# Cross-attention: both halves of the values product side by side, half of k a step ahead, v between the turns

## What is computed

```python
def _L0_xattn_ref(query, key_value, Wq, bq, Wk, bk, Wv, bv, Wo, bo):
    ...
    q = (query @ Wq + bq).reshape(B, Nq, H, D).transpose(0, 2, 1, 3)
    k = (key_value @ Wk + bk).reshape(B, Nkv, H, D).transpose(0, 2, 1, 3)
    v = (key_value @ Wv + bv).reshape(B, Nkv, H, D).transpose(0, 2, 1, 3)
    attn = jnp.einsum('bhqd,bhkd->bhqk', q, k) * scale
    ...
    attn = jax.nn.softmax(attn, axis=-1)
    x = jnp.einsum('bhqk,bhkd->bqhd', attn, v).reshape(B, Nq, Cq)
    return x @ Wo + bo
...
x = x + _L0_xattn_ref(_layernorm(x, axis=-1), ctx_768, ...)
```

## Time and profile before

| | us |
|---|---|
| median of 3 runs | 1132.66 |
| lowest and highest run | 1132.36, 1137.8 |
| the profiled execution: its time | 1139.23 |
| its span, first to last instruction | 1137.4 |
| busy in it: PE, PEld, DVE, ACT, POOL | 1018.0, 876.5, 782.9, 654.5, 689.1 |

### The profile page before, as it was taken

The page is one execution under the profiler, slowest core; times in us unless marked ns, Lnnn a source line. Parts: engine busy times, 40 slices in busy tenths (PEclk is TensorE's granted clock), DMA queues, the critical chain, the costliest instruction groups (busy, mean ns, idle before and its releaser), DMA issues. The chain is left out here.

```text
span 1137.4 us, 30097 instructions
## 1 busy us (share of the span) xinstructions
PE 1018.0 (89%) x9432; PEld 876.5 (77%) x9433; DVE 782.9 (69%) x2353; ACT 654.5 (58%) x1517; POOL 689.1 (61%) x813
## 2 busy tenths in 40 slices
PE   5899999999999998797999728999999537999998
PEld 3698999998999977686788516778887526998997
DVE  7576776677667776564666589766766486777784
ACT  3466666666676651534778577556665373444541
POOL 2487777777777780445899417776777203655443
PEclk9899999999999997899999759999999767999999
DMA  5221122212222112890000511233233348545601
GB/s 161 70 63 60 55 79 71 67 56 60 74 61 78 60 46 93 223 351 1 1 0 1 94 70 34 47 46 55 47 51 51 93 149 258 146 117 176 136 6 11
DMA packets 68551, 94.33 MB, mean 83 GB/s; under 512 B 12764, under 2 KB 48048, under 8 KB 68496
## 3 DMA queue, kind: packets, MB, share of 16 engines
q1 hardware_dynamic: 52464, 73.02, 20.2%
q0 software_dynamic: 16032, 20.62, 11.0%
HBM read 73.69 MB, written 22.18 MB: 84 GB/s over the span
## 5 line engine op out<-in xcount | busy, mean ns | idle before, releaser
L1921 POOL DMA_INDIRECT e_x<-rows,source x71 | 76.0, 1071 | 101.3 <-ACTq L1758 35.9
L652 ACT ACTIVATE xa_pr<-xa_pr,xa_nm 128x257 f32<-128x257 f32 x256 | 109.6, 500 | 21.7 <-DVE xa_nm L701 21.7
L635 ACT ACTIVATE xa_kT<-xa_kvp,xw_bk 128x258 fp32r<-128x258 f32 x128 | 60.8, 476 | 91.0 <-PE xa_kvp L465 83.7
L694 DVE TENSOR_SCALAR_CACHE_REDUCE xa_pr<-xa_sc 128x257 f32<-128x257 f32 x256 | 98.0, 421 | 13.6 <-PE xa_sc L490 9.0
L1932 POOL DMA_INDIRECT out_x<-e_y,target x32 | 54.0, 1688 | 77.3 <-DVE e_y L2719 65.5
L1926 POOL DMA_INDIRECT base<-e_y,place x39 | 76.7, 1968 | 35.5 <-DVE e_y L2209 21.9
L2610 ACT ACTIVATE e_h<-e_hb,rc_F_b 128x512 f32<-128x512 f32 x64 | 44.0, 688 | 91.1 <-PE e_hb L2556 90.4
L2556 PE MATMUL e_hb<-e_xTs,e_w1s 128*128 128x512 f32 x384 | 92.3, 401 | 1.9 <-issue 1.9
L597 POOL TENSOR_TENSOR xa_ol<-xa_om,xa_tl 128x256 f32<-128x256 f32 x64 | 46.6, 728 | 75.5 <-DVE xa_rinv L724 75.3
L2572 PE MATMUL e_yb<-e_w2s,e_hTs 128*128 128x256 f32 x768 | 89.5, 278 | 0.0
L705 DVE TENSOR_SCALAR xa_pT<-xa_ptp 128x512 f32<-128x512 f32 x128 | 87.3, 682 | 1.8 <-PE xa_ptp L500 1.6
(11 more groups left out here) (365 smaller groups left out, 3009.4 us busy)
## 6 DMA issues: line engine op xcount, KB each, us to landing
e_w<-in_F_W SPq DMA_DIRECT2D x16, 1024.0 KB
w<-in_W SPq DMA_DIRECT2D x24, 512.0 KB, 9.8
xa_ctx<-in_ctxT SPq DMA_DIRECT2D x32, 257.0 KB, 3.2
xa_ctx<-in_ctxT SPq DMA_DIRECT2D x64, 128.5 KB, 3.2
xa_vb<-vlx SPq DMA_DIRECT2D x64, 128.0 KB
rows<-xs_oT SPq DMA_DIRECT2D x4, 516.0 KB, 10.0
xs_oT<-in_x SPq DMA_DIRECT2D x4, 512.0 KB, 4.1
base<-xs_oT SPq DMA_DIRECT2D x4, 512.0 KB, 3.2
```

The source lines that it names most:

```text
L652: act.activation(pr[:, par, g, :], pr[:, par, g, :], ACT.Exp, bias=nm[:, par, g:g + 1], scale=-1.0).then_inc(exp_ready, 1)
L694: dve.tensor_scalar(pr[:, par, g, :], sc[:, g, 0:S], CLAMP, None, ALU.min, ALU.min, accum_out=mx[:, par, g:g + 1]).then_inc(clip_ready, 1)
L1921: return pool.indirect_dma_start(out=out, out_offset=None, in_=rows, in_offset=bass.IndirectOffsetOnAxis(ap=index, axis=0))
```

## The change

On every engine the change reorders what a step does, and leaves the work the same.

- PE: `project_k` does one half a call. Half 1 of k(b+1) stands right behind the scores, half 0 of k(b+2), a step ahead, behind the second turn; `project_v(b+1)` stands between the two turns; `turn_output` and both halves of `values` then stand in one block before the next scores.
- ACT: only half 1 of `high_k(b+1)` ahead of the exponentials; half 0 of `high_k(b+2)` last.
- DVE: all four `clip` instructions in one block, then `store_output`, `bounds`, and behind them the copies of the probabilities and `rest_k`.
- POOL: `rest_of_context(b+2)` moves from the end of the step to right behind `normalise`, ahead of the queries.
- k(1) half 0 is projected, split and stored ahead of the first step. SP's list is the same.

```diff
--- before.py
+++ after.py
@@ -447,22 +447,21 @@
         def _(pe):
             pe.wait_ge(w.loaded, w.total)
 
-            def project_k(b, par):
-                pe.wait_ge(ch_ready, b * 2 + 2)
-                pe.wait_ge(cr_ready, b + 1)
+            def project_k(b, par, h):
+                if h == 0:
+                    pe.wait_ge(ch_ready, b * 2 + 2)
+                    pe.wait_ge(cr_ready, b + 1)
+                    pe.wait_ge(kh_ready, b * 2)
+                    pe.wait_ge(kl_ready, b * 2)
+                else:
+                    pe.wait_ge(v_ready, b)
                 high, rest = cs[:, par, 0], cs[:, par, 1]
-                for h in range(2):
-                    if h == 0:
-                        pe.wait_ge(kh_ready, b * 2)
-                        pe.wait_ge(kl_ready, b * 2)
-                    else:
-                        pe.wait_ge(v_ready, b)
-                    out, c = kvp[:, (par + h) % 2, 0:SE], slice(P * h, P * h + P)
-                    pe.matmul(out, wks[:, 0, c], high[:, 0, :], start=True, stop=False)
-                    pe.matmul(out, wks[:, 0, c], rest[:, 0, :], start=False, stop=False)
-                    pe.matmul(out, wks[:, 1, c], high[:, 0, :], start=False, stop=False)
-                    pe.matmul(out, wks[:, 2, c], high[:, 1, :], start=False, stop=False)
-                    pe.matmul(out, wks[:, 3, c], rest[:, 1, :], start=False, stop=True).then_inc(kp_ready, 1)
+                out, c = kvp[:, (par + h) % 2, 0:SE], slice(P * h, P * h + P)
+                pe.matmul(out, wks[:, 0, c], high[:, 0, :], start=True, stop=False)
+                pe.matmul(out, wks[:, 0, c], rest[:, 0, :], start=False, stop=False)
+                pe.matmul(out, wks[:, 1, c], high[:, 0, :], start=False, stop=False)
+                pe.matmul(out, wks[:, 2, c], high[:, 1, :], start=False, stop=False)
+                pe.matmul(out, wks[:, 3, c], rest[:, 1, :], start=False, stop=True).then_inc(kp_ready, 1)
 
             def project_v(b, par):
                 pe.wait_ge(kh_ready, b * 2 + 1)
@@ -527,28 +526,31 @@
 
             def step(b, par, slot):
                 scores(b, par)
+                if not static(b) or b < B - 1:
+                    project_k(b + 1, 1 - par, 1)
                 if not static(b) or b >= 1:
                     turn(b - 1, 1 - par, 0)
                 if not static(b) or b < B - 1:
-                    project_k(b + 1, 1 - par)
+                    project_v(b + 1, 1 - par)
                 if not static(b) or b >= 1:
                     turn(b - 1, 1 - par, 1)
+                if not static(b) or b < B - 2:
+                    project_k(b + 2, par, 0)
                 if not static(b) or b >= 2:
                     turn_output(b - 2, par)
                 if not static(b) or b >= 1:
                     values(b - 1, 1 - par, (2 * slot + par + 3) % 4, 0)
-                if not static(b) or b < B - 1:
-                    project_v(b + 1, 1 - par)
-                if not static(b) or b >= 1:
                     values(b - 1, 1 - par, (2 * slot + par + 3) % 4, 1)
 
             pe.wait_ge(wh_ready, 6)
             pe.wait_ge(wl_ready, 4)
             pe.wait_ge(rows_zeroed, 2)
-            project_k(0, 0)
+            project_k(0, 0, 0)
+            project_k(0, 0, 1)
             pe.matmul(ptp[0:B, 0:D], cl[:, 0, :], wv[:, 0, :], start=True, stop=False)
             pe.matmul(ptp[0:B, 0:D], cl[0:64, 1, :], wv[0:64, 1, :], start=False, stop=True).then_inc(vlp_ready, 1)
             project_v(0, 0)
+            project_k(1, 1, 0)
             run_steps(pe, step, 0, B)
             turn(B - 1, 1, 0)
             turn(B - 1, 1, 1)
@@ -603,6 +605,8 @@
             def step(b, par, slot):
                 if not static(b) or b >= 2:
                     normalise(b - 2, par)
+                if not static(b) or b < B - 2:
+                    rest_of_context(pool, o, b + 2, par, 1 - slot)
                 if not static(b) or b >= 1:
                     pool.wait_ge(exp_ready, b * 4)
                 if not static(b) or b < B - 1:
@@ -610,8 +614,6 @@
                 if not static(b) or b >= 1:
                     last_probability(b - 1, 1 - par)
                     last_value(b - 1, 1 - par, (2 * slot + par + 3) % 4)
-                if not static(b) or b < B - 2:
-                    rest_of_context(pool, o, b + 2, par, 1 - slot)
                 if static(b):
                     c = b if b < 4 else b - B + 8
                     x = xs[:, T // 8 * c:T // 8 * c + T // 8, :]
@@ -663,16 +665,18 @@
                 if not static(b) or b < B - 2:
                     high_context(b + 2, par, 1 - slot)
                 if not static(b) or b < B - 1:
-                    high_k(b + 1, 1 - par, 0)
                     high_k(b + 1, 1 - par, 1)
                 exponentials(b, par)
                 if not static(b) or b < B - 1:
                     store_v(b + 1, 1 - par, (2 * slot + par + 1) % 4)
+                if not static(b) or b < B - 2:
+                    high_k(b + 2, par, 0)
 
             act.wait_ge(ones_ready, 4)
             high_k(0, 0, 0)
             high_k(0, 0, 1)
             store_v(0, 0, 0)
+            high_k(1, 1, 0)
             run_steps(act, step, 0, B)
 
         @block.vector
@@ -735,24 +739,25 @@
                     mask_output(b - 2, par)
                     invert(b - 2, par)
                 clip(b, par, 0)
+                clip(b, par, 1)
                 if not static(b) or b >= 3:
                     store_output(b - 3)
+                bounds(b, par)
                 if not static(b) or b >= 1:
                     store_probabilities(b - 1, 1 - par, 0)
-                clip(b, par, 1)
                 if not static(b) or b < B - 1:
-                    rest_k(b + 1, 1 - par, 0)
-                bounds(b, par)
+                    rest_k(b + 1, 1 - par, 1)
                 if not static(b) or b >= 1:
                     store_probabilities(b - 1, 1 - par, 1)
-                if not static(b) or b < B - 1:
-                    rest_k(b + 1, 1 - par, 1)
+                if not static(b) or b < B - 2:
+                    rest_k(b + 2, par, 0)
 
             rest_k(0, 0, 0)
             rest_k(0, 0, 1)
             dve.wait_ge(vlp_ready, 1)
             dve.tensor_tensor(vl[:], ptp[0:B, 0:D].unsqueeze(1).to_broadcast([B, 4, D]), maskj[:],
                               ALU.mult).then_inc(vl_ready, 1)
+            rest_k(1, 1, 0)
             run_steps(dve, step, 0, B)
             mask_output(B - 2, 0)
             invert(B - 2, 0)
```

## The result

| | before | after |
|---|---|---|
| median of 4 runs | 1134.31 us | 1172.33 us (1171.54 to 1173.55) |
| ratio | | 1.034, interval 1.031 to 1.037 |
| profiled execution | 1139.23 us | 1172.67 us, span 1170.9 |
| scores to scores, median step | 5.945 us | 6.606 us |
| scores of step 3 to scores of step 63 | 359.4 us | 398.5 us |

A forecast was written before the change was run, and what follows sets the result against it. PE sets the time in the cross-attention: 5.70 us a step without waits plus 0.90 of waiting makes 6.60 against 5.96, + 38 us over 59 steps. Against the median of 1132.66 that gives 1171 us, range 1161 to 1184.

The forecast's parts named there:

- The wait: Second turn on PE: waits 0.90 us a step for the copy behind `bounds`, held by POOL's low part of the context.
- Rows 7 and 8: Profile rows before the change: two long `bounds`, each beside a long POOL instruction and ending 0.02 us behind it.
- PE without waits: PE's step if nothing waits: 5.70 us, 0.26 less than today, 15 us at most over 59 steps.
- The sum: Whole cross-attention step: 5.70 + 0.90 = 6.60 us against 5.96, + 38 us over 59 steps, 1171 us.
- The third rival: PE's clock falls too because PE idles: some 30 us more, 1200 us; chance 0.05.
- The first rival: `bounds` on DVE gets through unheld and the change pays: step 5.79 to 5.89, 1125 us; chance 0.08.
- The point of no loss: Length of `bounds` on DVE, 0.35 us, below which the change was forecast to gain.
- The second rival: `bounds` held for a part only: for half the wait, step near 6.1, 1140 to 1160 us; chance 0.07.
- k at 4.59: Half 0 of k on PE, due at 4.59 us into the step, waits 0 to 0.1 for `rest_k`; taken as 0.

The follow-up runs named there:

- e1_accum: Changed kernel with `bounds` in the form of tensor_scalar that also writes an accumulator into a spare tile, nothing moved; 1125.06 us, ratio 0.992.
- e8_copy_first: Changed kernel with accumulator-form `bounds`, first copy ahead of it, `store_output` behind `rest_k`, and on ACT half 0 of k ahead of storing v; 1113.27 us.
- e7_two_inputs: Changed kernel with `bounds` made by scalar_tensor_tensor reading the maxima twice from SBUF, same place; 1171.37 us, ratio 1.034.
- e4_pool_back: Changed kernel with POOL's list as before, the low part of the context last in the step; 1231.4 us, ratio 1.087.
- e6_accum_store: Changed kernel with accumulator-form `bounds` and `store_output` moved on DVE behind the first copy of probabilities and `rest_k`; 1127.01 us, ratio 0.994.
- e3_split: Changed kernel with POOL's low part of the context issued as two instructions of 128x257 instead of one of 128x514; 1138.92 us, ratio 1.006.

## Why the prediction was right

- **The wait.** Forecast: `bounds` ready at 2.4, POOL's low part until 3.36, copy at 3.31, turn at 4.15, 0.90 of waiting. Measured in the step shown: 2.45, 3.36, 3.30, 4.13 (238.83, with scores at 234.70), 0.88 against 3.25. The restart of 0.84 behind the copy holds also in `e1_accum` (216.42 to 217.25).
- **The rule and its proof.** Rows 7 and 8 were two of the three long instructions (over 0.3 us) out of 64; they gave the mechanism and its end to 0.02. The Trainium skill, SBUF — State Buffer, section Who interferes with whom, names it, and excepts the `tensor_scalar` that also writes out its accumulator; it has a `tensor_tensor` with both inputs in SBUF contend as well. The runs agree: 950 ns held, 157 in the form with an accumulator, 944 for the `scalar_tensor_tensor` with two inputs. That the thing shared is a port is what the page states; no run shows the port itself.
- **PE without waits.** Forecast 5.70 a step. The changed kernel never shows it, since its steps take 6.606. `e8_copy_first` does: 5.685, and against 5.945 that is 0.26 a step, the forecast's figure. Steps 3 to 63 take 343.2 us in it, 16.2 less than before, where the forecast had 15. The rule of TensorEngine Tiling (Array Packing), Key Properties in the Trainium skill, that a change of the tiling mode drains the array, agrees with the trace in sign; its gain was real and lay under a wait over three times as large.
- **The sum.** Forecast +38 us for the phase. Steps 3 to 63 gave 398.5 - 359.4 = +39.1, and the first three steps, counted as nothing, another 1.8 (19.40 instead of 17.61 us). Not all of this is the hold. In the profiled execution the third context landed late, ACT waited for it and PE for POOL's low part of it, and then the granted clock was at the lower of its two levels, 1.2 of 2.4 GHz, from 59.0 to 65.8 us (the last line is a window, with the columns of the earlier trace rows):

```profile
55.39 0.42 ACT L648 ACTIVATE xa_cs<-xa_ctx 128x257 fp32r<-128x257 f32 x1 [3.41 <-DMA xa_ctx<-in_ctxT]
57.75 0.36 PE L460 MATMUL xa_kvp<-xa_cs,xa_wks 128*128 128x258 f32 x1 [1.54 <-POOL xa_cs L127]
59.00:65.80 6.80, 6.80 (x60) 6.51 (x57) 4.48 (x18) 3.03 (x10) 5.95 (x9) 0.50 0.05 19
```

  The step from 60.41 took 8.07 us for it. `e7_two_inputs` has the same orders and the same hold and none of this: its first four steps take 25.2 us instead of 27.5, and its phase 38.7 us more than before, where the changed kernel's takes 40.9. So about 2.3 us of the 40.9 belong to the late context and the clock, and the forecast had neither. What is left of the first three steps is not clear of their scatter: with PE's old order they took 17.6, 18.0 and 18.3 us. Part of the closeness to 1171 is luck as well: the forecast starts from a median of 1132.66, and the table has 1134.31.
- **Around the phase.** The profiled execution of before was said to be a long one, and to stand 6.6 over the median. From the last scores to the end it took 719.3 us, and the eleven other kernels took between 709.0 and 714.9, the changed one 711.9. That is why the profiled times differ by 33 us only and the medians by 38. The clock there is 0.92 for 0.91.
- **The third rival** (the clock falls too) did not occur where it was feared: the granted clock is 1.00 from 65.8 to 440 us, with PE busy 89.19 of 100. But the clock did fall at the start of the phase, behind a wait of 1.54 us, for 6.8 us, and in `e4_pool_back`, where PE is busy 84.58 of 100, the clock is 0.95. So the rival was nearer than its chance of 0.05 says.
- **The first rival, priced 1125** for a free port, with a step of 5.79 to 5.89, did not occur, but its step was right: `e1_accum` is that case, at 1125.06 and 5.858. The time hits the price partly by luck, since `e6_accum_store`, with the same step, stands at 1127.01. The point of no loss was put too high, at `bounds` of 0.35 us: between 5.858 at 157 ns and 6.048 at 398 ns (`e3_split`) a straight line reaches 5.945 near 0.27 us, an estimate. The step of `e1_accum` is not 5.70, because the copy stands behind `store_output` and `bounds` and is 0.13 late for the turn. PE shows 99.7% busy there all the same, because a product counts as 0.28 us where the next follows after 0.12: a wait of 0.13 hides in that. `e8_copy_first`, which has no such wait, shows 99.6%. PE's busy share cannot show whether PE is the bound to better than this; the spacing of starts can.
- **The second rival** (held for a part) was seen only where it was made, in `e3_split` at 1138.92.
- **k at 4.59.** I took 0 from 0 to 0.1 for `rest_k`. Half 0 of k started 0.41 behind the turn (238.83 to 239.24), in `e8_copy_first` 0.35, so at most 0.06.

## What to carry to other kernels

A reorder is judged by what stands next to what on the other engines: a small DVE instruction of a few values that falls beside a long GpSimd instruction can be held until that instruction ends, and everything queued behind it that is due pays. Look at the longest of a group and not its median alone, and where they end; then change the form of the small instruction before changing the orders. Here one operand turned +3.4% into -0.8%, and a few small moves more made it -1.7%; some 3 us of each of these gains are not of the phase, and not explained.

## What the runs showed of the hardware that was not expected

- A hold does not appear as a wait. It is the duration of the held DVE instruction (950 for 160 ns), so DVE looked busier, 80.1 for 71.5%, for the same work.
- A small DVE instruction is not spared: four values a partition were held 0.95 us. Its form matters: `bounds` with an accumulator ran beside POOL at 157 ns. The clips (0.42 us) and `rest_k` (0.48 us) ran beside POOL at their usual length too, but they also take an input from PSUM.
- `bounds` ended 0.04 us behind POOL's instruction in the step shown (244.70 against 244.66; the median is 0.025), although POOL's next one was queued right behind it and started at 244.62. It did not have to wait for that one too. Splitting a POOL instruction is thus a way to shorten the hold (950 to 398 ns).
- `bounds` right behind the clip whose accumulator result it reads waited 0.15 us (`e6_accum_store`); independent work placed between was free.
- The copies of probabilities use the same operation on 128x512 out of PSUM and are not held: in `e1_accum` one runs from 216.42 to 217.11 under POOL's 215.93 to 217.23 in its usual 0.69 us. As far as these rows go, a hold takes the form and an input in SBUF. A bound with its maxima in PSUM was not tried.
